# An adaLN block on one core: four loads issued by ScalarE, one transfer per group of maxima, and new order tables

## The reference, cut to what matters

```
mod = (silu(c) @ wmod).reshape(32, 6, 1, 256)        # sa, ca, ga, sb, cb, gb
h = layernorm(x) * (1 + ca) + sa
q, k, v = split(h @ w_qkv.T + b_qkv)                  # 16 heads of 16
scores = q @ k.T / 4 + alibi_causal_mask              # per head, 512 x 512
x = x + ga * (softmax(scores) @ v @ w_out.T + b_out)
h = layernorm(x) * (1 + cb) + sb
p = softmax(h @ gate_W.T)                             # 8 experts
scale = count(p > 0.3) * p                            # counts fall on experts 0 and 1
x = x + gb * (sum_e scale_e * (h @ expert_W[e].T)) @ out_W.T
```

## Time and profile before

| | |
|---|---|
| median of three runs | 1619.7 us (1618.94 to 1621.8) |
| the profiled execution | 1623.59 us, its span 1621.6 us |
| busy | PE 91%, DVE 79%, ACT 72%, POOL 50%, PEld 58% |
| mean granted TensorE clock | 0.971 of full speed |
| chain that ended last | PE 53%, issue 12%, DVE 10%, DMA 10%, SP's queue 7%, POOL 6%, ACT 2% |

### The profile page before, as it was taken

How to read it: one execution, slowest core, us unless ns; L and a number is a source line. 1 busy time by engine, 2 the same in 40 slices (tenths; PEclk the granted TensorE clock), 3 DMA queues, 4 the chain that set the end, 5 groups by cost and what they waited for, 6 DMA issues and landing times.

```text
span 1621.6 us, 56230 instructions
## 1 busy us (share of the span) xinstructions
PE 1480.8 (91%) x21456; PEld 943.5 (58%) x21456; DVE 1281.8 (79%) x3074; ACT 1160.5 (72%) x2466; POOL 809.4 (50%) x871
## 2 busy tenths in 40 slices
PE   5788999999999999999999999999999999999874
PEld 4455566656656566566556666655565665666542
DVE  4577788888888888888878888887878887888732
ACT  0277777877777778777777877777777777787651
POOL 1112446664554566545455664545466444456445
PEclk8799999999999999999999999999999999999887
DMA  3245555545545545455554545555544455554430
GB/s 114 92 132 161 151 165 154 159 137 163 171 150 180 166 146 161 135 163 159 167 166 150 164 146 152 174 154 172 152 144 145 156 167 151 166 165 139 139 90 30
DMA packets 198737, 241.07 MB, mean 149 GB/s; under 512 B 24030, under 2 KB 148902, under 8 KB 198470
## 3 DMA queue, kind: packets, MB, share of 16 engines
q1 hardware_dynamic: 198476, 237.48, 48.3%
HBM read 135.06 MB, written 101.81 MB: 146 GB/s over the span
## 4 chain that ended last, share of the span: by engine, by line
PE 53%; issue 12%; DVE 10%; DMA 10%; SPq 7%; POOL 6%; ACT 2%; POOLq 0%; DVEq 0%; ACTq 0%
PE ps L508 19%; PE ps L607 9%; PE ps L659 7%; PE ps L602 6%; PE ps L654 5%; DMA xa<-in_L_attn_x 4%; DVE mxp L881 4%; DMA qk_d<-qk_st 3%; DVE qk_st L813 3%; PE ps L622 2%; SPq L364 2%; PE ps L524 2%; DVE zr L893 2%; DMA qs<-negm 1%; SPq L366 1%
## 5 line engine op out<-in xcount | busy, mean ns | idle before, releaser
L881 DVE TENSOR_REDUCE mxp<-ps 128x4 f32<-128x512 f32 (+1 forms) x1536 | 832.1, 592 | 108.9 <-PE ps L622 106.0
L688 ACT ACTIVATE prob<-ps 128x512 f32<-128x512 f32 (+1 forms) x1536 | 703.1, 524 | 94.0 <-PE ps L607 86.5
L622 PE MATMUL ps<-kz,qs 49*128 49x128 f16 (+1 forms) x4096 | 407.5, 232 | 0.0
L607 PE MATMUL ps<-qs,kz 50*128 50x128 f16 (+2 forms) x3584 | 402.1, 241 | 3.3 <-DVE mxp L881 1.6
L1021 POOL TENSOR_TENSOR om<-oc,rz 128x512 f32<-128x512 f32 x64 | 80.0, 1271 | 569.4 <-issue 543.2
L607 PEld LDWEIGHTS ps<-qs,kz 50*128 50x128 f16 x3584 | 263.7, 95 | 87.2 <-issue 24.5
L622 PEld LDWEIGHTS ps<-kz,qs 49*128 49x128 f16 x4096 | 287.7, 95 | 3.4 <-DVE mxp L881 1.3
L602 PE MATMUL ps<-mk 64*128 64x256 bf16 x1024 | 200.6, 276 | 59.2 <-DMA qs<-negm 36.7
L659 PE MATMUL ps<-prob,va 128*32 128x384 f32 (+2 forms) x3072 | 236.7, 380 | 0.0
L654 PE MATMUL ps<-prob,va 128*32 128x128 f32 x4096 | 209.0, 276 | 0.6 <-DVE qk_st L813 0.6
L618 PE MATMUL ps<-mk 64*128 64x256 bf16 x1024 | 201.8, 278 | 7.3 <-DMA kz<-qk_d 5.1
(11 more groups left out here) (119 smaller groups left out, 2813.8 us busy)
## 6 DMA issues: line engine op xcount, KB each, us to landing
qk_d<-qk_st SPq DMA_DIRECT2D x128, 256.0 KB, 3.0
ou_d<-ou SPq DMA_DIRECT2D x128, 256.0 KB, 2.3
qs<-qk_d SPq DMA_DIRECT2D x256, 96.0 KB, 2.4
kz<-qk_d SPq DMA_DIRECT2D x256, 96.0 KB, 2.4
xa<-in_L_attn_x SPq DMA_DIRECT2D x32, 512.0 KB, 5.0
qk_d<-qk_st SPq DMA_DIRECT2D x128, 128.0 KB, 3.3
xc<-in_L_attn_x SPq DMA_DIRECT2D x32, 512.0 KB, 4.8
oc<-ou_d SPq DMA_DIRECT2D x32, 512.0 KB, 5.0
```

The lines of the kernel that those rows point to most:

```text
L607: x_ = mm(bank[:, col:col + w * P], kz[rows, h // 2, kt * P:(kt + 1) * P], qs[rows, h // 2, qt * P:(qt + w) * P], start=(n > 0), stop=(n > ...
L622: x_ = mm(bank[:, col * P:(col + w) * P], qs[rows, h // 2, qt * P:(qt + 1) * P], kz[rows, h // 2, kt * P:(kt + w) * P], start=(n > 0), sto ...
L688: nc.scalar.activation(prob[:, h % 8, at:at + w], ps[:, ST + n, 0:w], ACT.Exp, scale=1.0 / FS).then_inc(s["exp_done"], 1)
L881: v.tensor_reduce(mxp[:, g % 2, at, first:first + apart * (BLOCKS[n] - 1) + 1:apart], bank.rearrange("p (m k) -> p m k", k=P), AX.X, ALU.m ...
```

## The change: who issues four loads, one transfer for the maxima, and the tables

1. `load_a`, `load_c`, `load_ga` and `load_gb` leave SP's queue and become steps of ScalarE, with the same waits and transfers. `load_a` stands in slot 14, `load_ga` and `load_gb` in slot 2, `load_c` in slot 5, behind the exponential of the slot's last part.
2. `load_aug` moves the 16 rows of `negm` with one transfer to two partitions of `qs`; it was one transfer per partition. The waits on `aug_loaded` count 16 and not 32.
3. All five tables and the banks of four steps are new.

```
-                for j in range(2):
-                    at = HALF * j + MX_ROWS
-                    sp.dma_start(qs[at:at + 1, 2 * g:2 * g + 2, :].rearrange("o a (t q) -> o (a t) q", t=QT),
-                                 negm[8 * j:8 * j + 8, :]).then_inc(s["aug_loaded"], 16)
+                sp.dma_start(qs[MX_ROWS::HALF, 2 * g:2 * g + 2, :].rearrange("j a (t q) -> j (a t) q", t=QT),
+                             negm[:]).then_inc(s["aug_loaded"], 16)
...
-            def load_a(b, _):
-                wait(sp, "xna_ready", b * QT)
-                sp.dma_start(xa[:], x[b].rearrange("(t p) d -> p t d", p=P)).then_inc(s["xa_loaded"], 16)
+            def load_a(b, _):
+                wait(act, "xna_ready", b * QT)
+                act.dma_start(xa[:], x[b].rearrange("(t p) d -> p t d", p=P)).then_inc(s["xa_loaded"], 16)
+
+            def load_c(b, _):
+                wait(act, "xg_ready", b)
+                act.dma_start(xc[:], x[b].rearrange("(t p) d -> p t d", p=P)).then_inc(s["xc_loaded"], 16)
...
 PE_AT = {
-    9: [(0, "mt", 3, 0), (0, "qk", 3, 1), (3, "moe", 1, -2)],
+    8: [(0, "qk", 2, 1), (0, "qk", 3, 1), (1, "mt", 3, 0)],
```

More of the change, by code:

```diff
@@ L48 @@
         ("pv", 0): 0, ("pv", 1): 1, ("pv", 2): 0, ("pv", 3): 1}
 ACT_AT = {
[L50 to L61, removed]
+    0: [(2, "hf_a", 0, 1)],
+    1: [(0, "hh_a", 0, 1), (2, "negm", 1, 0), (3, "hf_a", 1, 1)],
+    2: [(0, "hh_a", 1, 1), (0, "load_ga", 0, -1), (2, "ou", 3, -1), (2, "load_gb", 0, -2)],
+    3: [(1, "qk_hi", 0, 1), (2, "qk_hi", 1, 1), (3, "hf_c", 0, -2), (3, "hh_c", 0, -2), (3, "hf_c", 1, -2)],
@@ L62 @@
+    4: [(0, "hh_c", 1, -2), (2, "vst", 0, 1)],
+    5: [(1, "negm", 2, 0), (3, "load_c", 0, 0), (3, "gate_exp", 0, -2)],
+    6: [(3, "ou", 0, 0)],
+    7: [(2, "z0", 0, -2), (3, "qk_hi", 2, 1)],
+    8: [(0, "qk_hi", 3, 1), (1, "negm", 3, 0)],
+    9: [(3, "oh", 0, -1)],
+    10: [(0, "z0", 1, -2), (2, "ou", 1, 0)],
+    11: [(3, "z0", 2, -2)],
+    12: [(0, "oh", 1, -1)],
+    13: [(0, "vst", 1, 1), (3, "negm", 0, 1)],
+    14: [(2, "z0", 3, -2), (2, "load_a", 0, 3), (3, "ou", 2, 0)],
 }
 DVE_AT = {
-    0: [(3, "ot", 1, -2)],
@@ L65 @@
[L65 to L74, removed]
@@ L78 @@
+    8: [(0, "qk_lo", 2, 1), (0, "bn_a", 1, 2)],
+    9: [(2, "qk_lo", 3, 1)],
+    10: [(0, "bn_a", 2, 2), (2, "bn_a", 3, 2), (2, "ag_a", 0, 2), (3, "zs", 1, -2)],
+    12: [(2, "rmax", 0, 1)],
+    13: [(0, "zs", 2, -2)],
+    14: [(0, "ol", 0, -1), (1, "ol", 1, -1)],
+    15: [(0, "zs", 3, -2), (3, "ot", 0, -1)],
 }
 POOL_AT = {
-    0: [(0, "hl_a", 0, 2), (0, "hl_a", 1, 2), (0, "norm_c", 0, -1), (0, "xg", 0, 0), (0, "hl_c", 0, -1),
-        (0, "hl_c", 1, -1), (0, "spread", 3, 1), (0, "om", 0, 0), (0, "om", 1, 0), (0, "finish", 0, -1)],
@@ L82 @@
[L82 to L85, removed]
+    0: [(0, "hl_a", 0, 2), (0, "hl_a", 1, 2), (0, "norm_c", 0, -1), (0, "spread", 3, 1), (0, "hl_c", 0, -1),
+        (0, "hl_c", 1, -1), (0, "xg", 0, 0), (0, "om", 0, 0), (0, "om", 1, 0), (0, "finish", 0, -1),
+        (0, "norm_a", 0, 3)],
+    1: [(0, "spread", 0, 2), (0, "spread", 1, 2)],
+    2: [(0, "finish", 1, -1), (0, "x1", 0, 0), (0, "spread", 2, 2)],
@@ L86 @@
+    4: [(0, "x1", 1, 0)],
 }
 SP_AT = {
[L88 to L93 removed]
@@ L96 @@
+    3: [(0, "load_o", 0, 1)],
+    6: [(0, "store_rz", 0, 1)],
 }
@@ L436, in store_res @@
                 sp.dma_start(out[b].rearrange("(t p) d -> p t d", p=P), res[:]).then_inc(s["res_stored"], 16)
-            steps = dict(load_stack=load_stack, store_ou=store_ou, load_gb=load_gb, load_aug=load_aug, load_c=load_c,
-                         store_qk=store_qk, load_a=load_a, load_z=load_z, load_o=load_o, load_ga=load_ga, store_rz=store_rz,
-                         load_rz=load_rz, store_res=store_res)
+            steps = dict(load_stack=load_stack, store_ou=store_ou, load_aug=load_aug, store_qk=store_qk, load_z=load_z,
+                         load_o=load_o, store_rz=store_rz, load_rz=load_rz, store_res=store_res)
             def one(i):
@@ L771, in _ @@
             steps = dict(hf_a=hf_a_, hh_a=hh_a_, hf_c=hf_c_, hh_c=hh_c_, qk_hi=qk_hi, vst=vst_, negm=negm_, z0=z0_,
-                         ou=sums_out, gate_exp=gate_exp, oh=o_hi)
+                         ou=sums_out, gate_exp=gate_exp, oh=o_hi, load_a=load_a, load_c=load_c, load_ga=load_ga,
+                         load_gb=load_gb)
             iterations(act, one)
```

59 lines of the change are left out of this document (30 added, 29 removed), and 13 rows, old and new, of the table PE_AT.

## The result

The changed kernel took 1610.6 us (median of 12 runs, 1605.7 to 1624.3), the kernel before 1624.3 us beside it. The ratio is 0.994, 95% interval 0.991 to 0.996: some 10 us gained by the ratio (14 between the two medians), where 34 were forecast. The time lies in the range that was given (1566 to 1626), but not in the likeliest case's own (1570 to 1606). The profiled execution took 1621.2 us, which is among the longer ones of this kernel; it is read here for where time goes, and a second profile of the same kernel, at 1606.8 us, stands beside it where amounts matter.

What follows compares the result with a forecast made beforehand. TensorE, busy for 91% of the span, was taken as the bound. The terms -49.9 + 15.5 + 6 - 6 = -34.4 us took the median from 1619.7 to 1585 us (likeliest case, 46%, own range 1570 to 1606); the range was 1566 to 1626.

Steps and rivals of the forecast that it cites:

- So I take the whole wait at slot 8 as gone: TensorE's wait at slot 8 for the maxima vanishes, with `mt`'s and a third of VectorE's maxima wait: -49.9 us.
- the loads' leaving SP's queue: On SP, ahead of slot 8's row of maxima: loads taken out bring it 0.4 to 2.1 us sooner, taken as 1.4.
- The `qk` step: TensorE's second `qk` step goes ahead of slot 8's wait, giving the row of maxima 1.3 us more time.
- the row of maxima stays late: Rival at slot 8: one transfer lands much later or `xc` runs into the reload; 1600 us or no gain, 13%.
- The 10.5 us of `mt`: TensorE's wait before `mt` for VectorE's `qk_lo`, 21 cases, counted as gone within the -49.9 us.
- The excess in the issues: SP's 1.07 and 1.37 us issues, 0.68 and 0.98 us too long behind 512 KB loads; both excesses taken to go.
- Slot 9's wait for the exponential: TensorE at slot 9 waits 0.5 us more for slot 8's exponential in 31 iterations: +15.5 us, bounds 0 to +37.
- The second `t2`: Moved before slot 4, it waits for `qk_lo`: 0.2 us net in 31 iterations, +6 us, within 0 and +19.
- The clock: TensorE's clock drops after standing at slot 8 cost 9.3 us; two thirds come back, -6 us, within 0 and -9.
- One transfer: One issue for slot 8's maxima saves 0.63 us; by the skill's rule landing costs 0.44, leaving 0.2 net.
- Issues on ScalarE: Four load issues of 0.45 us each, 1.8 us an iteration on ScalarE, costed at nothing.
- The rival in which ScalarE becomes the bound: Slots 2 to 6: issues of 1.2 us make the kernel slower, +0.5 us in 31 iterations, 1635 us; 19%.

Runs made afterwards that it cites:

- both moves: Kernel after, with the store of `rz` behind the first two stores of the projection and the load of `xc` in slot 12: 1586.7 us, ratio 0.975 to before.

## Why the prediction was wrong

*The step that failed* is "So I take the whole wait at slot 8 as gone", the largest term, -49.9 us, with the 1.4 us that it took from the loads' leaving SP's queue. The `qk` step gives its 1.3 us. But the loads and the tables bring the row 0.6 us by the median and 0.1 by the mean, not 1.4, and the single transfer some 0.35. The term also compared one gain with the shown waits and took no account of scatter. In the two profiles of the kernel after, 26.1 and 14.6 us of the waits for the row and `kz` are left. What keeps them is the load of `xc`: it was issued 3.4 us ahead of the last store, and on a queue of its own it is issued between 0.8 us ahead of it and 0.8 behind. With it moved away, the waits fall to 5.9 us. The prediction named this load in its rival "the row of maxima stays late", with 13%, but set it against the reload, and against the return of the two long issues; it is the stores that it meets. The size was too small as well: alone, this part of the change costs 41 us (the loads on ScalarE in the kernel before), and putting the load elsewhere brings 57 back.

*The 10.5 us of `mt`* in the same term were misread. They are the idle time of two queues, of which only the second row is TensorE's matmuls; the first is the weight load (PEld), whose busy and idle time lies beside theirs:

```profile
PEld ps L560 <- DVE qk_st L813: 6.3, 11, 0.7
...
PE ps L560 <- DVE qk_st L813: 4.3, 10, 0.5
```

So the term could give 4.3 us there, 6.2 less than it took.

*The excess in the issues* was wrongly explained. The 1.07 and 1.37 us of the earlier trace rows were put down to the 512 KB loads ahead of them in the queue. SP's timeline shows that the store of `rz` stands between the load of `xc` and the first of them, and takes the usual time:

```profile
828.24 0.39 SPq L422 DMA_DIRECT2D xc<-in_L_attn_x  x1
828.88 0.51 SPq L412 DMA_DIRECT2D rz_d<-zr  x1
```

With the loads gone from SP's queue, such issues are still there (1.60 us above, up to 1.93 for L362). Worked out from the records of the trace, between 150 and 1500 us: all 49 of SP's issues over 0.9 us in the kernel after, and 56 of 65 in the kernel before, overlap an instruction packet of 8 KB or more, and the nine others are issues of `xa`, of 0.90 to 1.16 us; of the shorter ones it is about one in eight and one in ten. Both of the earlier trace rows are among them (packets from 828.87 to 830.19 and from 835.70 to 836.65). It is a coincidence of records, and no run took the fetching away.

*The rest of the sum comes out near, by errors that cancel.* Where slot 8 doesn't wait (the store of `rz` moved) the kernel takes 1587.9 us, and the forecast for the kernel after was 1585. Against the profile of before, TensorE's waits are lower by 35.6 (row of maxima), 9.4 (exponentials), 4.3 (`mt`) and 2.7 us (`kz`), and higher by 16.7 (`t2`) and 3.1 (VectorE's maxima): -32.2 in all. Its busy time is 3.0 us less, and the span 35.3 us shorter. So even there slot 8, `mt` and the maxima gave 12 us less than the 49.9 (-35.6, -1.1 for `kz` at slot 8, -4.3 and +3.1), and the exponential, which was to cost 15.5 us, cost nothing. That the two nearly cancel is luck. Term by term:
- *Slot 9's wait for the exponential*, +15.5 us: it did not come. Waits for `prob` fell from 13.0 to 4.0 us, those for `mxp` rose by 1.6. The term is +1.6 us at most.
- *The second `t2`*, +6: 16.6 us at `t2`, and the 9.0 that slot 5 no longer waits for the exponential given back, +7.6. Moving it back gained 6.4 us, though by no wait that the list shows.
- *The clock*, -6: not in the kernel after, where the stretch with the late slot 8 above is at 0.93 and the mean is 0.967 (0.970 in the second profile). With slot 8 free (the store of `rz` moved) it rose from 0.971 to 0.974 in the mean, and TensorE's busy time fell by 3.0 us.
- *One transfer*: its issue takes 0.54 us. From the end of the issue to slot 8's start, where that waited, it takes 1.11 us with two transfers (26 cases) and 1.6 with one (10 cases, 1.55 to 1.63 in the other kernels). So it lands 0.5 us later. From the start of the first issue to the end of the last it is 1.40 us before and 0.55 now, so the net gain at the row is some 0.35 us. The Trainium skill's rule ("DMA: Bandwidth & Descriptors", "Why a DMA increments its semaphore by 16 and not by 1") spreads a transfer over the largest number of engines up to 16 that divides the slowest dimension on both sides, two here. The trace agrees: the row's 16 packets of 256 B run as two chains of eight, one behind another, where each transfer of the pair has eight side by side. But the estimate of 0.44 us that was worked out from it is near by luck. It took 63 ns for a packet, and these follow at 14 ns, so that the chains take some 0.14 us against 0.08; the rest of the 0.5 us passes after the last packet, 0.78 us to TensorE's start and not 0.39, and no run explains it. Those 0.35 us an iteration, 11 us in sum, are worth 9 us in the kernel before, but 26 in the kernel after and 7 with both moves. The worth of a saving on this chain depends on how many iterations stand just over the threshold, and the pair is late at slot 0 too.
- *Issues on ScalarE*, 0.45 us each: 0.39, 0.41 and 0.345 us by their medians. The rival in which ScalarE becomes the bound falls: ScalarE's busy share is unchanged, and where the loads don't meet the stores the same four issues gain 16 us.

*The store of `rz`* was not in the prediction at all. It waits for VectorE 2.9 us in every iteration of the kernel after, with the critical stores behind it. The diff moves it from slot 3 to slot 6 in SP's table and leaves it ahead of the stores, as it was before; but before, the load of `xc` ahead of it held the stores anyway. To name what is queued behind a waiting instruction would have found it. What it costs in the kernel after is known from the move alone, 28 us.

*The other side of the sum*, by medians: the loads on ScalarE take 41 us (1666.7), the new tables give back 25 (1641.9 with loads and tables), and the single transfer gives 26 (1616.4). These are worths in this order; taken alone in the kernel before, the single transfer gives 9. The 25 of the tables are about what the `qk` step alone is worth, 22 us. A change of three parts with a net gain of 10 us had a part in it that cost four times as much.

## What to carry to other kernels

Read a wait that falls in most iterations as a distribution, not as a mean: a gain on a chain is worth what it takes off the iterations over the threshold, and something that only widens the scatter can take all of it back. Before a load is given to another engine's queue, look up what it will run beside: in one queue it was issued well ahead of the critical stores, in two it is issued among them, and its slot counts for more than who issues it. And in a queue that feeds a critical reload, put nothing that waits for another engine ahead of the stores.
